# Issuing GpSimd's row transfers without waits on TensorE's steps and without waits for landings

## The chip, the cores and the metric

The kernel runs on one core of a Trainium2 chip. Its time is the device time of one execution, in microseconds (us). Three runs of the kernel before gave 802.45, 809.31 and 810.42 us; their median, 809.31 us, is the time before.

## What is computed

The input x holds 16 sequences of 256 rows with 128 features. Four stages follow one another, each added to x and each fed with a layer norm of x:

```
x = x + attn_a(layernorm(x))      # one head of width 128: softmax(q k^T / sqrt(128)) v, then w_o
x = x + ffn(layernorm(x))         # mixture of experts, layer 0
x = x + attn_b(layernorm(x))      # 16 heads of width 8, causal, with biases
x = x + ffn(layernorm(x))         # mixture of experts, layer 1

# ffn, over N = 4096 rows, E = 8 experts, capacity = 1280 rows an expert
logits = x @ router_w;  gates = softmax(logits)
first and second choice of each row; its place in an expert is a running count over the rows
expert_in = the rows of each expert;  h = silu(expert_in @ w1 + b1);  expert_out = h @ w2 + b2
out = gated sum of a row's two expert rows + 0.1 * (silu(x @ sw1 + sb1) @ sw2 + sb2)
```

## The kernel before

Each engine has a program of its own, written out by hand. The engines meet at semaphores, and each engine works through its list in order, so that a wait holds up all that stands behind it on the same engine.

**The rows.** The 4096 rows are 32 tiles of 128 (`NT`). A pair is two sequences, so four tiles, and there are eight pairs (`PAIRS`). Routing is done pair by pair: VectorE takes the statistics of the second norm (`stats2_end`, L1464), GpSimd makes the inverse deviation (`rstd2_of`, L561 and L563), VectorE writes the normed rows to `xr` (`norm_r`, L1476), TensorE transposes them (`r_transpose`, L808) and makes the logits (L815), VectorE finds both choices (`lead`, `second`), TensorE counts (`counts`, L826 to L836), and VectorE writes the slot numbers (`placed`, L1543 to L1555).

**The row transfers.** `dispatch(l, k)` is GpSimd's indirect DMA (L580): it sends one tile of 128 rows to the slots in `x_slots`, in DRAM, that `slot_u` names. Each pair has eight (four tiles, two choices), so each layer has 64, numbered k from 0 to 63. At every eighth it waits for `placed` of that pair. At the fifth of each eight it waits until the first-choice rows of the pair before have landed.

**Attention A.** TensorE, ScalarE and VectorE go through rounds, a pair in each (`attn_a_pair`). In round i the rows of pair i-2 get their places. GpSimd's list for the rounds 2 to 7 is in `attn_a`: seven transfers a round (four in round 2), each behind a wait for a step of TensorE in that round (`probs_tr` L788, `gv_done` L771, `y_done` L798), and then `rstd2_of(i + 1)`, whose result the next steps of VectorE need. This leaves 25 of the 64 transfers for the time after the attention.

**The layer of experts.** `moe` has items of 256 rows. The first ten in layer 0 and nine in layer 1 (`FRONT`) are pieces of the shared part, which take nothing from `x_slots`. Behind them come 40 chunks of the experts. SyncE's `chunk_loads` waits for all 64 transfers to land, and only then loads the first five chunks into `xg` (L370). TensorE transposes a chunk (`x_tr`, L889), VectorE splits it into a high and a low part (`x_split`, L1662 and L1664), and TensorE multiplies (`first_mm` L918, `second_mm` L939).

**Waits for landings.** `landed(l, k)` holds GpSimd until transfer k is in DRAM. `bursts(l, first, upto, size)` puts one behind every `size` transfers: in layer 0 from transfer 39 to 47 in fours, that is behind 42 and behind 46. In layer 1, where GpSimd is busy with the causal masks until transfer 39 and then sends 40 to 63, they stand behind 42 and behind 47 (`landed(1, 6 * 8 - 1)`), and `rstd2_of(2 * PAIRS)`, the norm of the last pair, stands behind 43.

Of the kernel before, what the change touches and what calls it, by code (L numbers as in the profile page):

```python
# [16 lines left out]
SEQS, SEQ, D = 16, 256, 128  # L17
T = SEQS * SEQ
NT = T // P
PAIRS = SEQS // 2  # L20
# [65 lines left out]
def build(nc, x_in, hd_mask, w_q, w_k, w_v, w_o, attn_W, attn_b, out_W, out_b, router_w,  # L86
          w1, b1, w2, b2, sw1, sb1, sw2, sb2, out):
    with ExitStack() as ctx:
# [93 lines left out]
        S = Signals()  # L182
# [121 lines left out]
        slots2 = (S.slots2_even, S.slots2_odd)  # L304
# [160 lines left out]
        def _(pool):  # L465
# [31 lines left out]
            def key_masks():  # L497

                rows = bdk[96:P, 0, 0, 0, 0:P]
                pool.memset(rows.bitcast(F32), -2.0 ** (KEY_EXP + STEP * SPAN)).then_inc(S.key_mask, 1)  # L500

                for m in range(SPAN, 0, -1):
                    pool.wait_ge(S.key_mask, SPAN - m + 1)
                    pool.affine_select(out=rows, in_=rows, compare_op=ALU.is_ge, pattern=[[1, P]], channel_multiplier=-SPAN,
                                       base=4 * SPAN - m, fill=-2.0 ** (KEY_EXP + STEP * (m - 1)) if m > 1 else 0.0).then_inc(S.key_mask, 1)
                pool.wait_ge(S.key_mask, SPAN + 1)
                pool.affine_select(out=rows, in_=rows, compare_op=ALU.is_ge, pattern=[[0, P]], channel_multiplier=1,
                                   base=-4, fill=0.0).then_inc(S.key_mask, 1)
                pool.wait_ge(S.key_mask, SPAN + 2)
                pool.tensor_copy(bdk[96:P, 0, 0, 0, P:SEQ], rows).then_inc(S.key_mask, 1)  # L510
                pool.wait_ge(S.key_mask, SPAN + 3)
                pool.tensor_copy(bdk[96:P, 0, 0, 1:4, :], bdk[96:P, 0, 0, 0:1, :].broadcast_to([32, 3, SEQ])).then_inc(S.key_mask, 1)
                pool.wait_ge(S.key_mask, SPAN + 4)

            def key_ones():

                for j in range(4):
                    pool.affine_select(out=bdk[96:P, 0, 0, j, :], in_=bdk[96:P, 0, 0, j, :], compare_op=ALU.not_equal,
                                       pattern=[[0, SEQ]], channel_multiplier=1, base=-j, fill=1.0).then_inc(S.key_mask, 1)
                    pool.wait_ge(S.key_mask, SPAN + 5 + j)  # L520

            def query_masks():

                rows = qc[96:P, 0, 0, 0:P]
                pool.memset(rows.bitcast(F32), 0.0).then_inc(S.query_mask, 1)
                for l in range(SPAN):
                    pool.wait_ge(S.query_mask, l + 1)
                    pool.affine_select(out=rows, in_=rows, compare_op=ALU.not_equal, pattern=[[1, P]], channel_multiplier=-SPAN,
                                       base=4 * SPAN - l, fill=2.0 ** (QUERY_EXP - STEP * l)).then_inc(S.query_mask, 1)
                pool.wait_ge(S.query_mask, SPAN + 1)  # L530

            def rstd_of(q, n):

                pool.wait_ge(S.ln_mv, n)
                pool.tensor_scalar(ve[:, 4 * q:4 * q + 4], mv[:, 4 * q:4 * q + 4, 1], EPS, 1.0, ALU.add, ALU.mult).then_inc(S.ln_ve, 1)
                pool.wait_ge(S.ln_ve, n)
                pool.tensor_tensor(rstd[:, 4 * q:4 * q + 4], ve[:, 4 * q:4 * q + 4], neg_half[:, :], ALU.pow).then_inc(S.ln_rstd, 1)
# [18 lines left out]
            def rstd2_of(n):  # L556
                pool.wait_ge(S.ln2_mv, n)
                if n > PAIRS + 1:

                    pool.wait_ge(S.xn2_ready, n - 1)  # L560
                pool.tensor_scalar(ve2[:, :], mv2[:, :, 1], EPS, 1.0, ALU.add, ALU.mult).then_inc(S.ln2_ve, 1)  # L561
                pool.wait_ge(S.ln2_ve, n)
                pool.tensor_tensor(rstd2[:, :], ve2[:, :], neg_half[:, :], ALU.pow).then_inc(S.ln2_rstd, 1)  # L563

            def dispatch(l, k):

                q, c, j = k // 8, k % 8 // 4, k % 4
                n, t = PAIRS * l + q, 4 * q + j
                if k % 4 == 0:
                    if c == 0:  # L570
                        pool.wait_ge(S.placed, PLACED * (n + 1))
                    elif n > 0:

                        pool.wait_ge(slots2[(n - 1) % 2], 64 * ((n - 1) // 2 + 1))
                if k == 0:
                    if l == 0:
                        pool.wait_ge(S.slots_zeroed, 16)
                    else:
                        pool.wait_ge(S.xg_tr, NCH)
                pool.indirect_dma_start(x_slots, bass.IndirectOffsetOnAxis(ap=slot_u[:, c, t:t + 1], axis=0),  # L580
                                        xr[:, t, :], None, bounds_check=E * CAP - 1, oob_is_err=False
                                        ).then_inc(S.slots1 if c else slots2[n % 2], 16)

            def landed(l, k):

                q, c, j = k // 8, k % 8 // 4, k % 4
                n = PAIRS * l + q
                if c:
                    pool.wait_ge(S.slots1, 512 * l + 64 * q + 16 * (j + 1))
                else:  # L590
                    pool.wait_ge(slots2[n % 2], 64 * (n // 2) + 16 * (j + 1))

            def bursts(l, first, upto, size):

                for k in range(first, upto):
                    dispatch(l, k)
                    if (k - first) % size == size - 1 and k + 1 < upto:
                        landed(l, k)

            def scatter(l, c):  # L600
                g = NCH * l + c
                pool.wait_ge(S.yo_ready, item_of_chunk(l, c) + 1)
                pool.wait_ge(S.row_set, g + 1)
                if c == 0:
                    if l == 0:

                        pool.wait_ge(S.bdk_zeroed, 16)
                    else:
                        pool.wait_ge(S.y_used, PAIRS)
                for j in range(CH):  # L610
                    pool.indirect_dma_start(y_rows, bass.IndirectOffsetOnAxis(ap=row_cur[:, g % ROWS, j:j + 1], axis=0),  # L611
                                            yo[:, g % RING, j, :], None, bounds_check=2 * T - 1, oob_is_err=False
                                            ).then_inc(sca[g % RING], 16)

            def attn_a():
                rstd_of(0, 1)
                pool.wait_ge(S.const_pool, N_CONST_POOL)
                pool.wait_ge(S.ln_rstd, 1)
                key_masks()
                rstd_of(1, 2)  # L620
                pool.wait_ge(S.ln_rstd, 2)
                key_ones()
                query_masks()
                for q in range(2, 7):
                    rstd_of(q, q + 1)
                rstd2_of(1)
                rstd_of(7, 8)
                rstd2_of(2)
                k = 0

                def row():
                    nonlocal k
                    dispatch(0, k)
                    k += 1


                for i in range(2, PAIRS):
                    n = 2 * i
                    if i > 2:
                        pool.wait_ge(S.probs_tr, n + 1)  # L640
                        row()
                        pool.wait_ge(S.gv_done, min(n + 3, SEQS))
                        row()
                    pool.wait_ge(S.y_done, n + 1)
                    row()
                    pool.wait_ge(S.probs_tr, n + 2)
                    row()
                    pool.wait_ge(S.gv_done, min(n + 4, SEQS))
                    row()
                    pool.wait_ge(S.y_done, n + 2)  # L650
                    row()
                    if i > 2:
                        row()
                    rstd2_of(i + 1)

                bursts(0, k, 6 * 8, 4)
                for k in range(6 * 8, 2 * NT):
                    dispatch(0, k)

            def attn_b_consts():  # L660
                pool.wait_ge(S.wb_in, 16 * WB_LOADS)
# [56 lines left out]
            for i in range(-1, PAIRS):  # L718
                k = attn_b_pair(i)

            rstd2_of(2 * PAIRS - 1)
            causal(PAIRS - 1, 1, GRP - 2)
            causal(PAIRS - 1, 1, GRP - 1)
            bursts(1, k + 1, k + 5, 3)
            rstd2_of(2 * PAIRS)
            for k in range(k + 5, 6 * 8):
                dispatch(1, k)
            landed(1, 6 * 8 - 1)
            for k in range(6 * 8, 2 * NT):
                dispatch(1, k)  # L730
            for c in range(NCH):
                scatter(1, c)
# [1322 lines left out]
```

## Time and profile before

| | |
|---|---|
| median of three runs | 809.31 us (802.45 to 810.42) |
| the profiled execution | 807.04 us, its span 805.3 us |
| TensorE matmuls | 724.6 us busy, 90% of the span, 6280 instructions |
| TensorE weight loads | 658.5 us, 82% |
| VectorE | 498.8 us, 62% |
| ScalarE | 444.4 us, 55% |
| GpSimd | 443.2 us, 55%, 564 instructions |
| row transfers, L580 | 128, 131.1 us, mean 1024 ns; idle before them 53.0 us |
| TensorE's granted clock, mean of the span | 0.964 of full speed |

The span is what the profiler saw from the first to the last instruction; the execution's own time is 1.7 us longer. Attention A fills the first 104 us or so, the experts of layer 0 stand between 104 and 317 us, attention B follows until about 591 us, and the experts of layer 1 run to the end. TensorE is busy for nine tenths of the span, so what matters is where it stands still, and for whom.

### The profile page before, as it was taken

Reading aid. Unit: us, or ns where it says so; the run is one execution under the profiler, and the core shown is the slowest. Engines: PE = TensorE matmul, PEld = TensorE weight load, DVE = VectorE, ACT = ScalarE, POOL = GpSimd, SP = SyncE. Lnnn points to the kernel's source line nnn. Section 1 sums busy time; section 2 is a strip of 40 time slices with the busy share of each in tenths; the row PEclk is TensorE's granted clock in tenths of the full one; section 3 lists DMA queues with packets and bytes.
Section 4 is the critical chain, followed back from the end, with each engine's and each line's share of the span. In section 5 each row is a group of like instructions: output and inputs, shape, how many; then the busy total and the mean of one; then the engine's idle time right before and its main releaser. Section 6 shows DMA issues by size and latency. Waiting matters only on the chain. (4 is left out here: it accounts for less than half of the span.)

```text
span 805.3 us, 18389 instructions
## 1 busy us (share of the span) xinstructions
PE 724.6 (90%) x6280; PEld 658.5 (82%) x6280; DVE 498.8 (62%) x1594; ACT 444.4 (55%) x1135; POOL 443.2 (55%) x564
## 2 busy tenths in 40 slices
PE   5888789699999997799999889999899799999994
PEld 4777689699999997577777677776689699999994
DVE  4877665245444446678888988877665345444437
ACT  2555345244444442587877877877555244444456
POOL 7367766155555562154454776776757155555530
PEclk9999869899999999899999999999989899999999
DMA  7896111233334223434423432333001233333138
GB/s 257 304 294 159 46 40 50 71 103 102 97 96 121 78 77 105 132 97 122 125 87 112 149 120 90 97 116 105 33 29 50 77 94 96 101 109 113 53 101 231
DMA packets 82723, 89.34 MB, mean 111 GB/s; under 512 B 13016, under 2 KB 70970, under 8 KB 82536
## 3 DMA queue, kind: packets, MB, share of 16 engines
q1 hardware_dynamic: 72432, 70.56, 29.8%
q0 software_dynamic: 9216, 17.34, 6.4%
q8 instruction: 51, 0.84, 0.4%
q10 hardware_dynamic: 984, 0.29, 0.2%
q14 instruction: 40, 0.33, 0.1%
HBM read 49.63 MB, written 39.67 MB: 111 GB/s over the span
## 5 line engine op out<-in xcount | busy, mean ns | idle before, releaser
L1277 ACT ACTIVATE hT<-bank,bias_T 128x256 f32<-128x256 f32 x448 | 175.4, 475 | 213.7 <-PE bank L918 213.7
L611 POOL DMA_INDIRECT y_rows<-yo,row_cur x160 | 157.7, 985 | 144.5 <-DVE yo L1787 117.7
L580 POOL DMA_INDIRECT x_slots<-xr,slot_u x128 | 131.1, 1024 | 53.0 <-issue 33.0
L1874 DVE TENSOR_REDUCE negp<-bank 128x2 f32<-128x512 f32 (+1 forms) x192 | 129.5, 685 | 46.2 <-PE bank L984 27.2
L939 PE MATMUL bank<-w_s,hT 128*128 128x128 f32 x1280 | 155.9, 275 | 0.0
L939 PEld LDWEIGHTS bank<-w_s,hT 128*128 128x128 f32 x1280 | 150.0, 192 | 0.0
L918 PE MATMUL bank<-xT_hl,w_hl 128*128 128x256 f32 x960 | 136.2, 292 | 1.1 <-DVE xT_hl L1664 1.1
L681 POOL TENSOR_SCALAR_AFFINE_SELECT pt<-pt 128x512 f32<-128x512 f32 x128 | 85.8, 678 | 92.8 <-ACT pt L1338 92.5
L1338 ACT ACTIVATE pt<-bank 128x512 f32<-128x512 f32 x192 | 107.7, 596 | 42.2 <-PE bank L1005 40.4
L1787 DVE TENSOR_TENSOR yo<-bank,b_b 128x256 f32<-128x256 f32 x80 | 33.9, 424 | 146.5 <-PE bank L939 146.5
L918 PEld LDWEIGHTS bank<-xT_hl,w_hl 128*128 128x128 f32 x960 | 121.5, 193 | 1.9 <-issue 1.9
L939 PE MATMUL bank<-sw_s,hT 128*128 128x128 f32 x512 | 64.1, 279 | 1.6 <-issue 1.4
L1024 PE MATMUL bank<-pt,v_ext 128*32 128x256 f32 (+1 forms) x1024 | 56.5, 339 | 8.2 <-POOL pt L681 8.1
L939 PEld LDWEIGHTS bank<-sw_s,hT 128*128 128x128 f32 x512 | 61.3, 196 | 2.4 <-issue 2.4
L918 PE MATMUL bank<-xT_hl,sw_hl 128*128 128x256 f32 x384 | 56.7, 300 | 2.9 <-issue 2.4
L918 PEld LDWEIGHTS bank<-xT_hl,sw_hl 128*128 128x128 f32 x384 | 51.0, 202 | 3.9 <-issue 3.2
L1024 PEld LDWEIGHTS bank<-pt,v_ext 128*32 128x32 f32 x1024 | 27.2, 111 | 29.9 <-POOL pt L681 11.6
L983 PE MATMUL bank<-bdk,qc 96*128 96x256 f32 x128 | 49.1, 383 | 0.9 <-DVE negp L1874 0.4
L1662 DVE CAST xT_hl<-bank 128x256 fp32r<-128x256 f32 x80 | 33.1, 414 | 17.9 <-PE bank L889 17.9
L979 PE MATMUL bank<-bdk,qc 128*128 128x512 f32 x64 | 31.5, 491 | 12.0 <-DMA qc<-qk_rows 11.8
L889 PE MATMUL bank<-ident,xg 128*128 128x128 f32 x160 | 31.6, 281 | 11.5 <-DMA xg<-x_slots 11.4
L1001 PE MATMUL bank<-qc,bdk 128*128 128x256 f32 x256 | 41.4, 284 | 0.0
(209 smaller groups left out, 1205.5 us busy)
## 6 DMA issues: line engine op xcount, KB each, us to landing
xg<-x_slots SPq DMA_DIRECT2D x80, 136.0 KB, 2.1
w_s<-in_L_ffn_w SPq DMA_DIRECT2D x32, 256.0 KB, 3.1
qk_rows<-qks SPq DMA_DIRECT2D x16, 512.0 KB, 3.7
bdk<-qk_rows SPq DMA_DIRECT2D x192, 32.0 KB
qc<-qk_rows SPq DMA_DIRECT2D x48, 128.0 KB, 2.9
x_slots<-xg SPq DMA_DIRECT2D x1, 5440.0 KB, 21.4
y_rows<-xg SPq DMA_DIRECT2D x1, 4096.0 KB, 15.7
yab<-y_rows SPq DMA_DIRECT2D x16, 256.0 KB, 3.4
```

The costliest lines, as they stand in the source:

```text
L580: pool.indirect_dma_start(x_slots, bass.IndirectOffsetOnAxis(ap=slot_u[:, c, t:t + 1], axis=0), xr[:, t, :], None, bounds_check=E * CAP - ...
L611: pool.indirect_dma_start(y_rows, bass.IndirectOffsetOnAxis(ap=row_cur[:, g % ROWS, j:j + 1], axis=0), yo[:, g % RING, j, :], None, bounds ...
L681: a = pool.affine_select(out=blk, in_=blk, compare_op=ALU.is_ge, fill=0.0, base=0, pattern=[[0, 4], [1, P]], channel_multiplier=-1)
L918: m = pe.matmul(bk[:, (f % 2) * 256:(f % 2) * 256 + 256], wt[:, wp, f * P:(f + 1) * P], xT_hl[:, w % 2, xp, :], start=(p == 0), stop=(p == 2))
L939: m = pe.matmul(yb(w, l)[:, j * P:(j + 1) * P], hT[:, w % 2, f, j * P:(j + 1) * P], wt[:, f, :], start=(f == 0), stop=(f == FT - 1))
L983: pe.matmul(halves[:, :, 0:P], q[0:96], heads[0:96, :, 0:P], start=True, stop=True)
L1001: m = pe.matmul(bk[:, j * SEQ:j * SEQ + SEQ], bdk[:, par, g, 2 * k + j, 0:P], qc[:, par, g, :], start=True, stop=True)
L1024: m = pe.matmul(OB[32 * j:32 * j + 32, c0 + kt * P:c0 + SEQ], v_ext[:, par, kt, 4 * g + j, :], rhs, start=(kt == 0 and g % 2 == 0), stop=( ...
L1277: a = act.activation(hT[:, w % 2, f, :], HB[2 * (w % 2) + f // 2][:, (f % 2) * 256:(f % 2) * 256 + 256], ACT.Silu, bias=bias_T[:, b0 + f:b ...
L1338: act.activation(pt[:, g % 2, k, :], CB[(g + k) % 2][:, :], ACT.Exp).then_inc(S.exp_done, 1)
L1787: dve.tensor_tensor(yo[:, g % RING, :, :], rows, b2_b[:, e:e + 1, :].broadcast_to([P, CH, D]), ALU.add).then_inc(S.yo_ready, 1)
L1874: dve.tensor_reduce(dst, AB[(g + k) % 2][:, :].rearrange("p (j k) -> p j k", j=heads), AX.X, ALU.max, negate=True).then_inc(S.amax_done, 1)
```

## The change

In attention A the seven transfers of a round follow one another, with no wait for TensorE between them; the number of transfers a round, and the place of `rstd2_of` behind them, stay. After the rounds, the remaining 25 transfers of layer 0 go out with no wait for a landing. In layer 1 both waits for landings go, and five transfers in place of four stand ahead of the last `rstd2_of`. The waits inside `dispatch` (for `placed`, and for the first-choice rows of the pair before) stay.

```diff
-            def landed(l, k):
...
-            def bursts(l, first, upto, size):
...
                 for i in range(2, PAIRS):
-                    n = 2 * i
-                    if i > 2:
-                        pool.wait_ge(S.probs_tr, n + 1)
-                        row()
-                        pool.wait_ge(S.gv_done, min(n + 3, SEQS))
-                        row()
-                    pool.wait_ge(S.y_done, n + 1)
-                    row()
-                    pool.wait_ge(S.probs_tr, n + 2)
-                    row()
-                    pool.wait_ge(S.gv_done, min(n + 4, SEQS))
-                    row()
-                    pool.wait_ge(S.y_done, n + 2)
-                    row()
-                    if i > 2:
+                    for _ in range(7 if i > 2 else 4):
                         row()
                     rstd2_of(i + 1)
-
-                bursts(0, k, 6 * 8, 4)
-                for k in range(6 * 8, 2 * NT):
-                    dispatch(0, k)
+                while k < 2 * NT:
+                    row()
...
             rstd2_of(2 * PAIRS - 1)
             causal(PAIRS - 1, 1, GRP - 2)
             causal(PAIRS - 1, 1, GRP - 1)
-            bursts(1, k + 1, k + 5, 3)
+            for k in range(k + 1, k + 6):
+                dispatch(1, k)
             rstd2_of(2 * PAIRS)
-            for k in range(k + 5, 6 * 8):
-                dispatch(1, k)
-            landed(1, 6 * 8 - 1)
-            for k in range(6 * 8, 2 * NT):
+            for k in range(k + 1, 2 * NT):
                 dispatch(1, k)
```

What GpSimd's list is in one round of attention A (round 3, transfers 4 to 10, and the norm behind them) before:

```order
L580 DMA x_slots<-xr,slot_u 10240x136 [waits probs_tr]
L580 DMA x_slots<-xr,slot_u 10240x136 [waits gv_done]
L580 DMA x_slots<-xr,slot_u 10240x136 [waits y_done]
L580 DMA x_slots<-xr,slot_u 10240x136 [waits probs_tr]
L580 DMA x_slots<-xr,slot_u 10240x136 [waits placed,gv_done]
L580 DMA x_slots<-xr,slot_u 10240x136 [waits y_done]
L580 DMA x_slots<-xr,slot_u 10240x136
L561 TENSOR_SCALAR ve<-mv 128x4 [waits ln2_mv]
L563 TENSOR_TENSOR rstd<-ve,neg_half 128x4 [waits ln2_ve]
```

And the same round in the changed kernel:

```order
L580 DMA x_slots<-xr,slot_u 10240x136 x4
L580 DMA x_slots<-xr,slot_u 10240x136 [waits placed]
L580 DMA x_slots<-xr,slot_u 10240x136 x2
L561 TENSOR_SCALAR ve<-mv 128x4 [waits ln2_mv]
L563 TENSOR_TENSOR rstd<-ve,neg_half 128x4 [waits ln2_ve]
```

The same seven transfers stand ahead of the same norm; of their waits only that for the places of the next pair is left.

GpSimd's list at the end of attention B, from transfer 40 of layer 1 (the first row) to transfer 51 (the last), before:

```order
L580 DMA x_slots<-xr,slot_u 10240x136 [waits placed]
L580 DMA x_slots<-xr,slot_u 10240x136 x2
L580 DMA x_slots<-xr,slot_u 10240x136 [waits slots2_odd]
L561 TENSOR_SCALAR ve<-mv 128x4 [waits xn2_ready,ln2_mv]
L563 TENSOR_TENSOR rstd<-ve,neg_half 128x4 [waits ln2_ve]
L580 DMA x_slots<-xr,slot_u 10240x136 [waits slots2_even]
L580 DMA x_slots<-xr,slot_u 10240x136 x3
L580 DMA x_slots<-xr,slot_u 10240x136 [waits placed,slots1]
L580 DMA x_slots<-xr,slot_u 10240x136 x3
```

And in the changed kernel, to transfer 51 as well:

```order
L580 DMA x_slots<-xr,slot_u 10240x136 [waits placed]
L580 DMA x_slots<-xr,slot_u 10240x136 x3
L580 DMA x_slots<-xr,slot_u 10240x136 [waits slots2_even]
L561 TENSOR_SCALAR ve<-mv 128x4 [waits xn2_ready,ln2_mv]
L563 TENSOR_TENSOR rstd<-ve,neg_half 128x4 [waits ln2_ve]
L580 DMA x_slots<-xr,slot_u 10240x136 x3
L580 DMA x_slots<-xr,slot_u 10240x136 [waits placed]
L580 DMA x_slots<-xr,slot_u 10240x136 x3
```

The waits on `slots2_odd` and `slots1`, which are those for the landing of transfers 42 and 47, are gone, and transfer 44 (the one that waits on `slots2_even`) has moved ahead of the norm.

## Rows read from the trace of the kernel before

**Rows 1.** Waits of TensorE over the whole span: total, times, longest in us.

```profile
PE bank L889 <- DMA xg<-x_slots: 11.4, 2, 6.1
```

**Rows 2.** Timeline of GpSimd, one round of attention A: start, duration, work [idle before].

```profile
49.75 0.20 POOL L561 TENSOR_SCALAR ve<-mv 128x4 f32<-128x4 f32 x1 [1.13 <-DVE mv L1464]
...
57.12 0.97 POOL L580 DMA_INDIRECT x_slots<-xr,slot_u  x1 [0.90 <-PE bank L771]
...
60.71 0.20 POOL L561 TENSOR_SCALAR ve<-mv 128x4 f32<-128x4 f32 x1
```

**Rows 3.** Timeline of TensorE: the counts, one set a round of attention A.

```profile
50.06 0.23 PE L826 MATMUL bank<-base_row,ones_bf 128*128 128x128 bf16 x1 [0.68 <-DVE acc L1534]
...
60.81 0.23 PE L826 MATMUL bank<-base_row,ones_bf 128*128 128x128 bf16 x1 [0.69 <-DVE acc L1534]
...
71.78 0.23 PE L826 MATMUL bank<-base_row,ones_bf 128*128 128x128 bf16 x1 [0.69 <-DVE acc L1534]
```

**Rows 4.** Timeline of VectorE at the statistics and norms of attention A.

```profile
49.28 0.38 DVE L1464 BATCH_NORM_AGGREGATE mv<-st 128x2 f32<-128x6 f32 x4
...
60.02 0.38 DVE L1464 BATCH_NORM_AGGREGATE mv<-st 128x2 f32<-128x6 f32 x4
...
62.06 0.35 DVE L1476 TENSOR_SCALAR xr<-x,mv,rstd 128x128 f32<-128x128 f32 x1 [0.46 <-POOL rstd L563]
...
62.85 0.52 DVE L1476 TENSOR_SCALAR xr<-x,mv,rstd 128x128 f32<-128x128 f32 x1
```

**Rows 5.** Timeline of GpSimd after attention A: transfers 42, 43, 47 and 63 of layer 0.

```profile
111.90 0.97 POOL L580 DMA_INDIRECT x_slots<-xr,slot_u  x1 [0.30 <-issue]
115.24 0.97 POOL L580 DMA_INDIRECT x_slots<-xr,slot_u  x1 [2.36 <-DMA x_slots<-xr,slot_u]
...
122.63 0.97 POOL L580 DMA_INDIRECT x_slots<-xr,slot_u  x1 [2.08 <-DMA x_slots<-xr,slot_u]
...
143.34 0.97 POOL L580 DMA_INDIRECT x_slots<-xr,slot_u  x1 [0.30 <-issue]
```

**Rows 6.** Timeline of TensorE at the first chunk of layer 0.

```profile
147.88 1.52 PE L889 MATMUL bank<-ident,xg 128*128 128x128 f32 x4 [6.10 <-DMA xg<-x_slots]
149.81 2.90 PE L918 MATMUL bank<-xT_hl,w_hl 128*128 128x256 f32 x12 [0.41 <-DVE xT_hl L1664]
```

**Rows 7.** Timeline of GpSimd, layer 1: transfer 43, the last norm, transfer 48.

```profile
594.71 0.96 POOL L580 DMA_INDIRECT x_slots<-xr,slot_u  x1 [2.10 <-DMA x_slots<-xr,slot_u]
595.75 0.20 POOL L561 TENSOR_SCALAR ve<-mv 128x4 f32<-128x4 f32 x1
...
604.91 0.96 POOL L580 DMA_INDIRECT x_slots<-xr,slot_u  x1 [2.08 <-DMA x_slots<-xr,slot_u]
```

**Rows 8.** The chain that ended last, layer 1: start, us, what.

```profile
624.65 2.28 DMA x_slots<-xr,slot_u
...
631.00 2.90 PE bank L918 x12
633.90 2.38 PE bank L939 x16
...
636.49 1.44 PE bank L918 x12
637.93 1.79 PE bank L939 x16
```

**Rows 9.** Timeline of VectorE: slot numbers of pair 7 (layer 0) and pair 6 (layer 1).

```profile
121.20 0.15 DVE L1555 TENSOR_TENSOR slot_u<-RR,far 128x4 uint32<-128x4 f32 x1
...
599.96 0.16 DVE L1555 TENSOR_TENSOR slot_u<-RR,far 128x4 uint32<-128x4 f32 x1
```

**Rows 10.** Windows: length, busy of PE, PEld, DVE, ACT, POOL, clock, DMA share, GB/s.

```profile
15.40:17.50 2.10, 0.01 (x1) 0.00 (x0) 2.06 (x13) 1.57 (x6) 1.48 (x6) 1.00 1.01 412
...
94.70:97.00 2.30, 1.79 (x15) 1.50 (x15) 2.06 (x11) 1.02 (x4) 2.07 (x2) 0.72 0.00 0
...
141.80:147.80 6.00, 0.00 (x0) 0.00 (x0) 0.00 (x0) 0.00 (x0) 1.95 (x2) 0.93 0.25 77
```

More of the change, by code:

```diff
@@ L582, in dispatch @@
                                         ).then_inc(S.slots1 if c else slots2[n % 2], 16)
-            def landed(l, k):
[L586 to L591, printed above, removed]
-            def bursts(l, first, upto, size):
[L595 to L598, printed above, removed]
             def scatter(l, c):
```

## The prediction

> **What bounds the kernel now.** I read the waits of TensorE first, since it is busy for 90% of the span. Two of its waits are for the load of a first chunk: 11.4 us in two pieces, 6.1 us in layer 0 and the other 5.3 us in layer 1 [rows 1]. Then the chain that ended last: in layer 1 it goes back from the end of the experts through the load to the landing of the last row transfer, and from there up GpSimd's list of transfers [rows 8]. So GpSimd's last transfer sets when the experts start, and behind the start TensorE runs with no gap until the tail. In layer 0 the same pattern stands in the timelines: transfer 63 is issued at 143.34 us, and TensorE starts the first chunk at 147.88 us after 6.10 us of standing still [rows 5, 6]. Last I looked at whether GpSimd also holds up the rounds of attention A, where its norm stands behind seven transfers.
>
> **Waits on TensorE's steps.** One of them costs: the fifth transfer of a round stands 0.90 us, where the usual gap is 0.30 us, so 0.60 us a round [rows 2, 5]. That is GpSimd's time, and it counts only if the norm behind the transfers is late. It is, a little: VectorE's statistics end at 60.02 + 0.38 = 60.40 us, and GpSimd starts the norm at 60.71 us, while in the round before, where GpSimd was waiting, it started 0.09 us after them (49.28 + 0.38 against 49.75) [rows 2, 4]. So it is 0.31 - 0.09 = 0.22 us late, and VectorE waits 0.46 us for it [rows 4]. TensorE's rounds show the same number: 60.81 - 50.06 = 10.75 us with a norm in time, 71.78 - 60.81 = 10.97 us with a late one [rows 3]. Without the 0.60 us GpSimd is ready at about 60.11 us, before the statistics, and the round is VectorE's and TensorE's again at 10.75 us. Three rounds have a late norm (starts at 60.71, 71.68 and 82.64 us); the last two rounds are paced by other work. Sum: 3 x 0.22 = 0.7 us. Bounds: 0 if the rounds find another pace at 10.97 us, 1.4 us if the 0.46 us of VectorE's wait went in all three. What is late next is the statistics.
>
> **Waits for landings, layer 0.** Transfer 43 stands 2.36 us and transfer 47 2.08 us [rows 5]. With the usual 0.30 us in their place, 2.06 + 1.78 = 3.84 us go. Nothing takes their place: the only wait left in this stretch that could come last is that of transfer 56 for the slots of pair 7, which are written at 121.20 us [rows 9], and transfer 56 goes out seven transfers ahead of 63, so at about 134 us before and 130 us after. The shared pieces of TensorE end at 147.88 - 6.10 = 141.78 us, and shift with attention A by the same 0.7 us as GpSimd does. So the standing still falls from 6.10 to 2.26 us, all 3.84 us are gained, and 2.26 us of cover are not there to be used up: had the saving been over 6.1 us, the rest would have been lost.
>
> **Waits for landings, layer 1.** Transfer 43 stands 2.10 us and transfer 48 2.08 us [rows 7]: 1.80 + 1.78 = 3.58 us. The transfer that is moved ahead of the last norm costs 1.27 us there (0.97 + 0.30), against the 1.80 us that are gone ahead of it, so the norm starts some 0.5 us earlier, and no later, than at 595.75 us. Transfer 48 would go out at about 601.3 us; the slots that it waits for are written at 599.96 us [rows 9], so this wait does not come up. TensorE's standing still falls from 5.3 to 1.7 us. The row transfers of both layers sum to 7.4 us.
>
> **The clock after the standing still.** In layer 0 the granted clock was at 1.00, and fell to 0.50 (1.2 GHz) near the end of the 6 us without a matmul (mean 0.93 over 141.8 to 147.8 us) [rows 10]. The first chunk then ran slowly: in layer 1 its two products took 2.90 and 2.38 us on the chain, the next chunk's 1.44 and 1.79 us, so 1.46 + 0.59 = 2.05 us more [rows 8]; layer 0 shows the same 2.90 us [rows 6]. If the clock stays at 2.4 GHz through 2.3 and 1.7 us, that comes back, about 1.9 us a layer (2.05, less since layer 0's second product overlaps a little more). At 15.4 us TensorE stood still for 2.10 us, and the clock was 1.00 throughout [rows 10]. Against it: in attention A it fell to a mean of 0.72 at 94.7 to 97.0 us, in a slack stretch [rows 10]; and here the transposes of the first chunk and VectorE's split follow the gap, in which TensorE does little for 1.93 us (147.88 to 149.81) [rows 6]. So the bounds are 0 and 4.1 us. I take both, 3.8 us, as the likeliest single case, being nearest to the row with the same length of gap.
>
> **The sum.** 0.7 + 3.84 + 3.58 + 3.8 = 11.9 us. The profiled execution took 807.04 us (span 805.3), which gives 795.1 us. The median of the runs lies 2.3 us higher, which gives 797.4 us by the same sum; I forecast 796. From the fastest run, 802.45, it would be 790.5.
>
> **A page against the trace.** A transfer starts behind each norm of GpSimd's, while VectorE norms the rows, and it shows: the third TENSOR_SCALAR took 0.52 us in place of 0.35 [rows 4]. The Trainium skill (SBUF — State Buffer, section "SBUF: two separate sides") says that GpSimd and VectorE's instructions in a two-port mode take a shared pair of ports as an exclusive lock, so that the loser stands until the other has ended. By that rule an instruction that meets a transfer would stand up to 0.97 us, and the sum would turn into the loss worked out under the third rival; by the row it stands 0.2 us, and the sum stays.
>
> **Rival 1: the clock falls all the same.** In both layers: 0.7 + 3.84 + 3.58 = 8.1 us, 799 us from the profiled execution and 801 from the median. In one layer: 10 us, 797 to 799. For it speak the slack stretch in attention A and the split behind the gap; against it the gap at 15.4 us.
>
> **Rival 2: the landing grows with the row.** If transfers sent back to back wait for one another in the DMA queue, the last lands no earlier and only attention A's 0.7 us is left: 806 to 808.5 us. For it: transfer 42 took 115.24 - 111.90 = 3.3 us until GpSimd went on [rows 5]. Against it: transfer 63 of layer 1, after fifteen others without such a wait, landed in 2.28 us [rows 8], so no queue had built up. The same time comes if the freed waits turn up again inside GpSimd's issue.
>
> **Rival 3: slower, because VectorE meets the transfers.** The waits keep the middle transfers of a round behind steps of TensorE, while VectorE works on PSUM; without them they may fall on its norms. A round has eight TENSOR_SCALAR of this kind, four for each norm. If each stood for half a transfer, 0.49 us, a round would be 3.9 us longer, five rounds 19.5 us, and the time would be 807 - 11.9 + 19.5 = 815 us. It turns the sign from 11.9 / 5 = 2.4 us a round, 0.3 us for each of the eight. The row of 0.52 us shows 0.17 us in one of four [rows 4], and GpSimd is sending for nine of eleven microseconds already, so there is little room for more meetings.
>
> **The chances.** Both clocks stay: 0.38. One falls: 0.27. Both fall: 0.15. Rival 2: 0.13. Rival 3: 0.07. The range takes in both ends of the clock's case from the fastest run to the median, 790 to 801, and a part of what lies between rival 1 and rival 2: 789.5 to 804. A measurement of this kernel can tell about 1%, 8 us, from no change. The first two cases are faster by more than that (0.65), a third of rival 1's double case too (0.05); the rest of it, rival 2 and a little of rival 3 are within 1% (0.25); slower by over 1% is 0.05.
>
> **What the changed profile would show.** Right: no transfer of layer 0 or 1 that waits on DMA by more than 0.3 us; GpSimd's waits on TensorE gone, and its norm waiting some 0.4 us for the statistics; TensorE's counts 10.75 us apart in four rounds; TensorE's waits for the chunk load at about 2.3 and 1.7 us; the first `first_mm` of the experts near 1.7 us where the clock stayed up. Wrong: gaps of 5 to 6 us ahead of the first chunk with an earlier last transfer (rival 2); transfers of more than 1.3 us or TENSOR_SCALAR of more than 0.6 us in many rounds, with rounds over 11 us (rival 3); a clock of 0.50 behind gaps of 2 us (rival 1). The prediction would also be wrong if the clock in attention A, which before shows a mean of 0.72 at 94.7 to 97.0 us [rows 10], falls at another place: more may hang on that than on the 0.7 us that the change brings there.

## The result and the profile after

| | |
|---|---|
| before, beside it on the same chip | 809.26 us, median of six (802.45 to 810.42) |
| changed | 796.36 us, median of six (795.37 to 800.91) |
| ratio | 0.986, 95% interval 0.983 to 0.989: 9.1 to 14.1 us faster; the medians are 12.9 us apart |
| profiled execution of the changed kernel | 800.91 us, span 799.2 us, the slowest of its six |

The forecast was 796.0 us with a range of 789.5 to 804. Since the profiled execution is the slowest of its six, its rows show less of the gain than the median. I read it in the order of the prediction: the waits of TensorE, attention A, the two ends of the row transfers, the clock.

Waits of TensorE over the whole span: total, times, longest in us. This answers to [rows 1], where the same wait was 11.4 us.

```profile
PE bank L854 <- DMA xg<-x_slots: 5.7, 2, 2.9
```

It has halved, and the chain that ended last still goes through it in layer 1. In the list of the costliest groups GpSimd's transfers are as long as before, and only the idle time ahead of them has shrunk, from 53.0 to 40.0 us; nearly all that is left is the usual gap between two of them (122 gaps, 34.3 us in all):

```profile
L580 POOL DMA_INDIRECT x_slots<-xr,slot_u x128 | 131.3, 1026 | 40.0 <-issue 34.3
```

Attention A, first GpSimd's timeline (start, duration, work, idle before), a round's last transfer and the norm behind it, as in [rows 2]:

```profile
61.09 0.97 POOL L580 DMA_INDIRECT x_slots<-xr,slot_u  x1 [0.30 <-issue]
62.51 0.20 POOL L561 TENSOR_SCALAR ve<-mv 128x4 f32<-128x4 f32 x1 [0.45 <-DVE mv L1429]
```

GpSimd now stands 0.45 us and waits for VectorE's statistics, where the norm was late before. TensorE's counts, as in [rows 3]:

```profile
52.08 0.23 PE L791 MATMUL bank<-base_row,ones_bf 128*128 128x128 bf16 x1 [0.69 <-DVE acc L1499]
...
62.83 0.23 PE L791 MATMUL bank<-base_row,ones_bf 128*128 128x128 bf16 x1 [0.69 <-DVE acc L1499]
...
73.58 0.23 PE L791 MATMUL bank<-base_row,ones_bf 128*128 128x128 bf16 x1 [0.70 <-DVE acc L1499]
```

They are 10.75 us apart, and so is the next. VectorE's norms, as in [rows 4], and behind them the transfer that GpSimd sends at that time:

```profile
63.87 0.35 DVE L1441 TENSOR_SCALAR xr<-x,mv,rstd 128x128 f32<-128x128 f32 x1 [0.24 <-POOL rstd L563]
...
64.65 0.52 DVE L1441 TENSOR_SCALAR xr<-x,mv,rstd 128x128 f32<-128x128 f32 x1
...
64.03 1.12 POOL L580 DMA_INDIRECT x_slots<-xr,slot_u  x1 [0.20 <-issue]
```

The wait for the norm fell from 0.46 to 0.24 us. Three of the four start inside the transfer's 1.12 us, at 64.32, 64.65 and 64.98 us: as before one of them took 0.52 us, the other two 0.34 us each.

GpSimd after attention A: the last norm of the stage, and transfer 63, as in [rows 5]. The first line is the same norm before:

```profile
106.22 0.20 POOL L561 TENSOR_SCALAR ve<-mv 128x4 f32<-128x4 f32 x1
...
107.63 0.20 POOL L561 TENSOR_SCALAR ve<-mv 128x4 f32<-128x4 f32 x1 [1.37 <-DVE mv L1429]
...
140.81 1.01 POOL L580 DMA_INDIRECT x_slots<-xr,slot_u  x1 [0.30 <-issue]
```

From the norm to transfer 63 it is 33.18 us; before, it was 143.34 - 106.22 = 37.12 us. No transfer between them waits for a landing. TensorE at the first chunk of layer 0, as in [rows 6]:

```profile
145.90 0.96 PE L854 MATMUL bank<-ident,xg 128*128 128x128 f32 x4 [2.77 <-DMA xg<-x_slots]
147.59 2.23 PE L883 MATMUL bank<-xT_hl,w_hl 128*128 128x256 f32 x12 [0.72 <-DVE xT_hl L1629]
...
152.45 0.38 PE L854 MATMUL bank<-ident,xg 128*128 128x128 f32 x2
```

Layer 1, GpSimd, as in [rows 7]: transfer 40 before, and then, of the changed kernel, transfer 40, the last norm, and two of the transfers that took longer than 0.97 us; transfer 63 starts at 617.53 us:

```profile
588.85 1.07 POOL L580 DMA_INDIRECT x_slots<-xr,slot_u  x1 [3.33 <-DVE slot_u L1555]
...
584.79 1.07 POOL L580 DMA_INDIRECT x_slots<-xr,slot_u  x1 [2.19 <-DVE slot_u L1520]
...
591.18 0.20 POOL L561 TENSOR_SCALAR ve<-mv 128x4 f32<-128x4 f32 x1
...
598.58 1.12 POOL L580 DMA_INDIRECT x_slots<-xr,slot_u  x1 [0.30 <-issue]
...
613.21 1.46 POOL L580 DMA_INDIRECT x_slots<-xr,slot_u  x1 [0.31 <-issue]
```

From 40 to 63 it is 32.74 us; before, it was 624.65 - 588.85 = 35.80 us. The chain that ended last (start, us, what), as in [rows 8]:

```profile
617.53 2.29 DMA x_slots<-xr,slot_u
...
619.83 2.19 DMA xg<-x_slots
...
623.76 2.90 PE bank L883 x12
```

and TensorE's own timeline there:

```profile
622.07 1.08 PE L854 MATMUL bank<-ident,xg 128*128 128x128 f32 x4 [2.88 <-DMA xg<-x_slots]
...
626.45 3.49 PE L904 MATMUL bank<-sw_s,hT 128*128 128x128 f32 x16
629.78 0.38 PE L854 MATMUL bank<-ident,xg 128*128 128x128 f32 x2
```

The landing takes 2.29 us as before (2.28), so in layer 1 nothing had queued up behind transfers sent back to back. The first chunk ran slowly in both layers. Windows of layer 0 and layer 1 (length, busy of PE, PEld, DVE, ACT, POOL, clock, DMA share, GB/s), as in [rows 10]:

```profile
143.50:147.00 3.50, 0.88 (x4) 0.41 (x4) 0.52 (x2) 0.00 (x0) 0.00 (x0) 1.00 0.58 166
147.00:150.00 3.00, 2.41 (x14) 2.44 (x15) 1.56 (x6) 0.15 (x1) 0.00 (x0) 0.73 0.38 108
622.00:624.00 2.00, 1.20 (x5) 0.68 (x6) 1.31 (x5) 0.00 (x0) 0.00 (x0) 0.71 0.66 202
624.00:627.00 3.00, 3.00 (x15) 3.00 (x16) 1.49 (x5) 0.31 (x1) 0.00 (x0) 0.50 0.30 73
```

In layer 0 the clock was at 1.00 until the first chunk's transposes had passed and fell within the next 3 us; in layer 1 it was at 0.50 (1.2 GHz) through the first product and the start of the second.

This execution by itself: from the first of TensorE's counts to the end of the span it took 799.2 - 41.38 = 757.8 us, before 805.3 - 39.36 = 765.9 us. That is 8.1 us less, the number of rival 1, and the clock fell in both layers, as in rival 1. But the pieces of the 8.1 us are not the terms of the forecast: 4.0 us go up to the first chunk of layer 0, 2.1 us from there to transfer 40 of layer 1, 2.9 us from that transfer to the first chunk of layer 1, and 0.9 us are lost behind it. The 2.1 us lie in the experts of layer 0 and in attention B, which the change doesn't touch. The nine traces of undisturbed sessions without a filling scatter from 434.9 to 442.4 us in that stretch, and their first count stands anywhere from 38.7 to 42.6 us; here it is 2.0 us later than before. So a single execution can't tell a term of 1 or 2 us by its total.

### The profile page after: what moved, and what is told of

The parts are those of the page before. It is cut to its first block and busy times, and to the rows that moved or that the text cites. A ratio compares the mean times of both kernels' runs of the same rounds, so it can differ in the third digit from the quotient of the medians.

```text
span 799.2 us, 18381 instructions
## 1 busy us (share of the span) xinstructions
PE 724.4 (91%) x6280; PEld 658.6 (82%) x6280; DVE 498.8 (62%) x1594; ACT 444.3 (56%) x1135; POOL 443.4 (55%) x564
## 5 line engine op out<-in xcount | busy, mean ns | idle before, releaser
L580 POOL DMA_INDIRECT x_slots<-xr,slot_u x128 | 131.3, 1026 | 40.0 <-issue 34.3
L1627 DVE CAST xT_hl<-bank 128x256 fp32r<-128x256 f32 x80 | 33.1, 414 | 11.6 <-PE bank L854 11.6
L948 PEld LDWEIGHTS bank<-bdk,qc 96*128 96x128 f32 x128 | 26.0, 203 | 17.3 <-issue 9.0
```

Of the source, the lines that this page charges most:

```text
L948: pe.matmul(halves[:, :, 0:P], q[0:96], heads[0:96, :, 0:P], start=True, stop=True)
```

## The experiments

Kernels that share a chip and a session share the runs of the kernel before. Their medians: first session 807.47 us (31 runs), second 827.88 (11), third 806.88 (11), fourth 806.55 (17).

### Each part alone

`e1_attn_a`: only the waits on TensorE's steps in attention A go.

```diff
-                    n = 2 * i
-                    if i > 2:
-                        pool.wait_ge(S.probs_tr, n + 1)
-                        row()
...
-                    pool.wait_ge(S.y_done, n + 2)
-                    row()
-                    if i > 2:
+                    for _ in range(7 if i > 2 else 4):
                         row()
```

> The kernel before with only attention A's waits on TensorE's steps removed. My theory (the parts add up): three rounds 0.22 us shorter, 0.7 us in all, which a measurement cannot tell from no change (ratio 0.999); in the profile GpSimd's norm waits some 0.4 us for the statistics, TensorE's counts stand 10.75 us apart in four rounds, and the standing still before the first chunk of layer 0 stays at 6.1 us. Rival (VectorE meets the transfers): rounds over 11 us, 1 us or more slower. Rival (these waits carried the gain): 4 us or more faster, with the standing still of layer 0 well under 6 us.

Measured: 807.66 us, ratio 1.000 (0.997 to 1.003). The same kernel on another chip in the fourth session:

> Attention A's part alone once more, for a chip where the kernel before takes some 828 us. Theory of the unbroken row (there, transfers that follow one another with nothing between them stall the other engines' issue after some five, and the waits on TensorE's steps keep the row broken): rounds 3 to 6 take 13 to 16 us in place of 11 to 12, some 15 us slower than before, ratio 1.015 to 1.02. Rival (on that chip the rows behind the attention do it): within 3 us of before, counts 11 to 12 us apart. On a chip where the kernel before takes 807 us: 1.000 again.

Measured: 808.57 us, ratio 0.999 (0.996 to 1.002). The traces have counts 10.75 us apart, so the mechanism is there, but its price is under what 24 runs can tell from nothing. The standing still ahead of the first chunk of layer 0, expected to stay at 6.1 us, was 7.51 us in the first and 6.12 us in the second.

`e2_land0`: only the waits for landings in layer 0 go.

```diff
-                bursts(0, k, 6 * 8, 4)
-                for k in range(6 * 8, 2 * NT):
-                    dispatch(0, k)
+                while k < 2 * NT:
+                    row()
```

> The kernel before with only the waits for landings of layer 0 removed. My theory: the standing still before the first chunk of layer 0 falls from 6.1 to 2.3 us, 3.8 us faster, and up to 5.7 where the clock stays up behind it (ratio 0.993 to 0.995); the last transfer lands 2.3 us after its issue. Rival (the landing grows with the row): nothing gained, the last transfer lands later after its issue.

Measured: 800.27 us, ratio 0.992 (0.989 to 0.995). The execution in the profile was the fastest of the twelve (795.54 us). TensorE at the first chunk of layer 0:

```profile
142.59 0.79 PE L888 MATMUL bank<-ident,xg 128*128 128x128 f32 x4 [2.38 <-DMA xg<-x_slots]
144.28 1.67 PE L917 MATMUL bank<-xT_hl,w_hl 128*128 128x256 f32 x12 [0.90 <-DVE xT_hl L1663]
...
147.58 0.38 PE L888 MATMUL bank<-ident,xg 128*128 128x128 f32 x2
```

Here the standing still is 2.38 us and the clock stayed: 1.67 us where before had 2.90. In layer 1 of the same execution, where the waits were kept, it is 5.33 us, and the product took 2.90 us:

```profile
617.72 1.12 PE L888 MATMUL bank<-ident,xg 128*128 128x128 f32 x4 [5.33 <-DMA xg<-x_slots]
619.65 2.90 PE L917 MATMUL bank<-xT_hl,w_hl 128*128 128x256 f32 x12 [0.82 <-DVE xT_hl L1663]
```

`e3_land1`: only the edit of layer 1, the last two pieces of the diff.

```diff
-            bursts(1, k + 1, k + 5, 3)
-            rstd2_of(2 * PAIRS)
-            for k in range(k + 5, 6 * 8):
+            for k in range(k + 1, k + 6):
                 dispatch(1, k)
-            landed(1, 6 * 8 - 1)
-            for k in range(6 * 8, 2 * NT):
+            rstd2_of(2 * PAIRS)
+            for k in range(k + 1, 2 * NT):
                 dispatch(1, k)
```

> The kernel before with only layer 1's part: its waits for landings removed, five transfers ahead of the last norm. My theory: the standing still of layer 1 falls from 5.3 to 1.7 us or, as in the changed kernel's profile, 2.9 us less what VectorE and TensorE give back; 3.6 us faster, up to 5.6 where the clock stays up (ratio 0.993 to 0.996). Rival (the moved transfer and the freed waits turn up in a wait for slot numbers): 1.8 us or less.

Measured: 801.19 us, ratio 0.992 (0.989 to 0.996). Its layer 1:

```profile
624.93 0.99 PE L887 MATMUL bank<-ident,xg 128*128 128x128 f32 x4 [1.48 <-DMA xg<-x_slots]
626.62 1.67 PE L916 MATMUL bank<-xT_hl,w_hl 128*128 128x256 f32 x12 [0.69 <-DVE xT_hl L1662]
```

`e10_landings_only`: both of these edits, attention A as before.

> The waits for landings of both layers removed, attention A's kept. On a chip where the kernel before takes some 828 us: rounds of attention A as before; by the theory of the unbroken row the pauses behind the attention begin earlier, and what the waits give is taken back there, within 4 us of before (0.995 to 1.005); if only attention A's part is harmful there, 7 us or more faster (0.990 or less). On a chip where the kernel before takes 807 us: 7.4 us and some clock, ratio 0.984 to 0.990.

Measured: 798.63 us, ratio 0.989 (0.984 to 0.994). The product of the three parts' ratios is 1.000 x 0.992 x 0.992 = 0.984, that of the whole 0.986, this one 0.989: they agree within their intervals, so the times show no more than a sum of the parts, and no share of attention A's. Its profile has both outcomes of the clock in one execution, layer 0 first:

```profile
145.28 0.99 PE L886 MATMUL bank<-ident,xg 128*128 128x128 f32 x4 [2.30 <-DMA xg<-x_slots]
146.97 1.67 PE L915 MATMUL bank<-xT_hl,w_hl 128*128 128x256 f32 x12 [0.70 <-DVE xT_hl L1661]
...
620.75 0.90 PE L886 MATMUL bank<-ident,xg 128*128 128x128 f32 x4 [2.79 <-DMA xg<-x_slots]
622.43 2.61 PE L915 MATMUL bank<-xT_hl,w_hl 128*128 128x256 f32 x12 [0.78 <-DVE xT_hl L1661]
...
627.27 0.38 PE L886 MATMUL bank<-ident,xg 128*128 128x128 f32 x2
```

### More of the suspected wait

`e6_more_landings`: the kernel before, with four waits for landings in place of two in layer 0.

```diff
-                bursts(0, k, 6 * 8, 4)
+                bursts(0, k, 6 * 8, 2)
```

> The kernel before with waits for landings behind every second transfer of layer 0's nine in place of every fourth: four waits in place of two. My theory (GpSimd's list is the chain, a wait costs 1.9 us): the standing still of layer 0 grows from 6.1 to 9.9 us, 3.8 us slower (ratio 1.005). Rival (a wait costs only where the queue is full, or is hidden): under 1 us.

Measured: 811.54 us, ratio 1.006 (1.003 to 1.008), so 4.4 us (2.0 to 6.8). In its trace GpSimd stands 2.09, 2.24, 2.09 and 2.08 us at the four waits, and TensorE 8.98 us ahead of the first chunk, against 6.10 [rows 6] and the 9.9 expected. Two more waits cost 4.4 us, near the 3.8 us that the forecast gives to two fewer, with the clock low behind the gap in both kernels (first product 2.90 us); this is the cleanest support for the main step.

### The changed kernel again, and the second session

`e0_after_again`: the changed kernel as it is.

> The changed kernel once more, beside the next kernels on one chip: ratio to the kernel before of 0.983 to 0.989 as in its own runs.

Measured: 840.85 us (832.86 to 846.87) against 827.88 (822.07 to 831.04) of the kernel before, ratio 1.014 (1.009 to 1.019). In the second session both kernels were slower than in any other, and the changed one was the slower of the two. One round of attention A, GpSimd:

```profile
71.46 0.97 POOL L580 DMA_INDIRECT x_slots<-xr,slot_u  x1 [0.30 <-issue]
77.90 0.20 POOL L561 TENSOR_SCALAR ve<-mv 128x4 f32<-128x4 f32 x1 [5.46 <-DVE mv L1429]
```

The transfers are as fast as ever, but the norm waits 5.46 us for the statistics; the counts stand at 50.10, 63.61, 79.04, 95.10 and 110.51 us, rounds of 13.5 to 16.1 us where the usual one has 10.75. The waits of TensorE, and below them its timeline in the pieces of the shared part:

```profile
PE bank L904 <- issue: 11.0, 14, 2.8
PE bank L883 <- issue: 10.0, 10, 1.9
```

```profile
136.34 0.55 PE L883 MATMUL bank<-xT_hl,sw_hl 128*128 128x256 f32 x3 [1.03 <-issue]
...
143.46 1.09 PE L904 MATMUL bank<-sw_s,hT 128*128 128x128 f32 x3 [1.03 <-issue]
```

TensorE runs a few matmuls and stands still for about a microsecond, over and over, and no engine or DMA that it waits for is shown ("issue"). In the usual profile the same two groups stand for 3.3 and 1.3 us in the whole span.

The wait for the first chunk does not occur in this execution, in neither layer. In layer 0 TensorE ends the shared pieces so late that it goes on to the chunk at 177.34 us without standing still, 17.0 us after transfer 63 (160.37 us); in the usual profiles the load is there 4.5 to 5.1 us after that transfer's start. What the earlier last transfer could give was not to be had here. The three other profiles of the session show no such wait either; the kernel before was not profiled in it.

`e7_rows_ahead` (changed kernel, 5, 7, 7, 7, 8, 8 transfers in the rounds in place of 4 and five times 7):

```diff
-                    for _ in range(7 if i > 2 else 4):
+                    for _ in range((5, 7, 7, 7, 8, 8)[i - 2]):
```

> The changed kernel with more transfers in the rounds of attention A: 5, 7, 7, 7, 8, 8 in place of 4, 7, 7, 7, 7, 7, so that 22 and not 25 are left behind it; GpSimd stood 1.9 us in round 2 and 1.4 us in round 7 waiting for the statistics. My theory (GpSimd's last transfer sets the start of the experts until the 2.8 us of standing still are used up): the standing still of layer 0 goes, 2.8 us less, and 1.6 us more from the clock; ratio to before 0.980 to 0.983. Rival (a transfer in a round delays the norm, and the rounds grow by 1 us each): no gain over the changed kernel or slower, with TensorE's counts more than 12 us apart in the last rounds.

Measured in the second session: 834.15 us, ratio 1.003 (0.998 to 1.009): in the disturbed session not told from the kernel before, and by the two ratios 1% better than the changed kernel (1.003 against 1.014).

`e4_after_fill` (changed kernel) and `e5_before_fill` (kernel before, with 44 in place of 16) keep TensorE multiplying the identity, into a bank that nobody reads, while it would stand still:

```diff
                     if c == -1:
+                        pe.wait_ge(S.yo_ready, ITEMS * l + 3)
+                        keep_busy(16)
                         x_tr(l, 0)
```

> The changed kernel with 16 matmuls of the identity on TensorE ahead of the first chunk's transposes in both layers (their result is written over), which fill most of the 2.8 us in which it stands still. Theory of the clock (what the change gained beyond the 8.1 us of waits is the clock that stays up in some executions; where it falls it costs 1.6 to 3 us a layer): the clock stays at 1.00 at both places, the first chunk's products take about 1.7 and 2.0 us, and the time is 1 to 4 us under the changed kernel's, near its fastest runs (795 us), with a narrower spread. Rival (the extra gain came from elsewhere): the same as the changed kernel within 0.5 us, though the clock stays up.

> The kernel before with 44 such matmuls at the same two places, filling most of the 6.1 and 5.3 us. Theory of the clock: 2 us less in each layer, some 4 us faster than the kernel before (ratio 0.995), at an unchanged standing time for the load. Rival (the clock's fall costs nothing, since the first chunk is bound by something else): no change.

Measured in the second session: 846.12 us, ratio 1.023 (1.019 to 1.027), and 851.66 us, ratio 1.030 (1.027 to 1.034). Neither tells of the clock here: in the second session there was no gap to fill, so that the filling came on top (3.6 us a layer in the one, 9.8 us in the other). But `e5_before_fill` has the waits of the kernel before, and its trace was taken beside that of the changed kernel: its counts go from 42.58 to 111.06 us in six rounds, 68.5 us, where those of `e0_after_again` go from 39.39 to 122.59 us, 83.2 us. The other two kernels without the waits of attention A agree with the latter: 82.5 us in `e4_after_fill`, 81.5 us in `e7_rows_ahead`. Yet TensorE pauses in `e5_before_fill` too. In layer 0 nearly all of it stands between 135 and 150 us, in the last transfers, which go out unbroken in both kernels; over the span its two groups of products stand for 26.9 us in 22 pauses, more than the 21.0 us of the changed kernel:

```profile
147.27 1.48 PE L939 MATMUL bank<-sw_s,hT 128*128 128x128 f32 x5 [3.25 <-issue]
```

### The same two in an undisturbed session

`e7b_rows_ahead`:

> The kernel with 5, 7, 7, 7, 8, 8 transfers in the rounds of attention A once more, hoping for a chip where the kernel before takes 807 us as in the first runs. My theory there: ratio to before 0.980 to 0.983, the standing still of layer 0 gone, TensorE's counts 10.75 us apart. If the chip is one where the kernel before takes some 828 us: near 1.003 again, with pauses of TensorE put down to issue.

Measured: 792.38 us (788.78 to 797.1) against 806.88, ratio 0.981 (0.977 to 0.984), the lowest ratio of all. Its interval just touches that of the changed kernel (0.983 to 0.989). Transfer 63 goes out at 138.16 us, and in layer 0 the wait for the chunk is all but gone:

```profile
143.78 0.44 PE L854 MATMUL bank<-ident,xg 128*128 128x128 f32 x2 [0.52 <-DMA xg<-x_slots]
144.50 1.67 PE L883 MATMUL bank<-xT_hl,w_hl 128*128 128x256 f32 x12 [0.29 <-DVE xT_hl L1629]
...
147.80 0.38 PE L854 MATMUL bank<-ident,xg 128*128 128x128 f32 x2
```

GpSimd's norm still waits 0.64, 0.46, 0.45, 0.45 and 0.15 us for the statistics in the rounds 2 to 6 and no longer in round 7: the rounds had room for just these three transfers.

`e4b_after_fill`:

> The changed kernel with 16 filling matmuls ahead of the first chunk in each layer once more. Theory of the clock, on a chip where the kernel before takes 807 us: the clock stays at 1.00 behind the gap in both layers, 1 to 4 us less than the changed kernel, ratio to before 0.981 to 0.986. Rival: 0.986 with the clock up, since the extra gain came from elsewhere.

Measured: 799.13 us, ratio 0.987 (0.984 to 0.991), where 0.981 to 0.986 was expected.

```profile
143.16 3.74 PE L704 MATMUL bank<-ident 128*128 128x128 f32 x32
146.73 0.60 PE L854 MATMUL bank<-ident,xg 128*128 128x128 f32 x4
148.36 1.66 PE L883 MATMUL bank<-xT_hl,w_hl 128*128 128x256 f32 x12 [1.03 <-DVE xT_hl L1631]
```

The clock stayed at 1.00 in both layers (1.66 us for the first product, in layer 1 too), so in this execution filling the gap was enough to keep it. The time did not fall below that of the changed kernel: the filling lasts 3.6 us to the first transpose, longer than the gap. The first chunk starts 146.73 - 139.37 = 7.4 us after the last transfer's start, against 145.90 - 140.81 = 5.1 us in the changed kernel; in layer 1 it is 5.1 against 4.5 us. Not all of the 2.3 us in layer 0 is the filling's doing: SyncE issued the load 4.28 us after the start of transfer 63, against 2.92 us in the changed kernel. The 0.6 to 2.3 us lost in a layer are of the size of what the clock gives back there (2.0 us, worked out below), and the runs, 794.0 to 801.5 us, scatter no less than those of the changed kernel.

## Why the prediction was right

**Waits for landings, layer 0.** Forecast 3.84 us, measured 37.12 - 33.18 = 3.94 us on GpSimd. By itself the part brings 6.5 us of time (ratio 0.992; 4.3 to 8.6), the wait and the clock together; the forecast for both was 5.7 us. The gap left was 2.77 us in the profiled execution, forecast 2.26; 2.30 and 2.38 us in two others. The 0.5 us lies behind transfer 63: from its start to the first transpose it is 145.90 - 140.81 = 5.09 us, before 147.88 - 143.34 = 4.54 us. SyncE issued the load 2.92 us after the transfer's start, before 2.41 us, and from the issue to the first transpose it is 2.2 and 2.1 us. Why the issue came later is open; in three other traces with the same transfers sent back to back (`e2_land0`, `e10_landings_only`, `e7b_rows_ahead`) it came after 2.40 to 2.46 us, so the missing waits alone don't explain it.

**Waits for landings, layer 1.** Forecast 3.58 us, measured 3.06: the waits are gone, but more transfers than before took 1.12 or 1.46 us in place of 0.97, as rows above show, and gave 0.5 us back. TensorE's pieces ended 0.5 us earlier too, counted from transfer 40, so the gap left was 2.88 us and not 1.7. With the same list it was 2.79 us in `e10_landings_only`, and 1.48 and 1.52 us in `e3_land1` and `e7b_rows_ahead`, where transfers 40 to 63 took 32.0 and 31.9 us. The part alone brings 0.992 (3.1 to 9.3 us); forecast 5.5.

**Attention A.** Forecast 0.7 us. The traces show the step: a norm that waits 0.45 us, counts at 10.75 us, 78.56 us from the first to the last count against 79.21. The time doesn't show it; two runs of the part alone gave 1.000 and 0.999.

**The clock.** The size of this term was right, and it went into the sum in full without being certain. I set 1.9 us a layer as if a gap of about 2 us kept the clock. The profiles, by the gap ahead of the first chunk: with 0.52, 1.48, 1.52, 2.30 and 2.38 us the first product took 1.67 us (clock at 2.4 GHz), with 2.77 us 2.23, with 2.79 us 2.61, and with 2.88 us 2.90; from 5.3 to 9.0 us it took 2.90 each time that it wasn't cut up in the record. What a kept clock gives back stands between the first chunk's transposes and those of the next chunk. Before:

```profile
154.88 0.38 PE L889 MATMUL bank<-ident,xg 128*128 128x128 f32 x2
...
629.06 1.23 PE L889 MATMUL bank<-ident,xg 128*128 128x128 f32 x4 [5.30 <-DMA xg<-x_slots]
...
636.11 0.38 PE L889 MATMUL bank<-ident,xg 128*128 128x128 f32 x2
```

So before it was 154.88 - 147.88 = 7.00 us in layer 0 and 7.05 us in layer 1. Where the clock stayed it is 147.58 - 142.59 = 4.99 us (`e2_land0`): 2.0 us a layer, the 1.9 forecast. Behind the three gaps of 2.77 to 2.88 us it is 6.55, 6.52 and 7.71 us, so the changed kernel's profiled execution won 0.4 us in layer 0, lost 0.7 us in layer 1 and got nothing of the term in all. All three gaps of that length were followed by a fall, so it isn't shown that the changed kernel ever kept the clock; its gap in layer 1 did vary by more than a microsecond in kernels with the same list there.

**The number.** The median gained 12.9 us, or 11.6 by the ratio, and the sum was 11.9. That the two are so near is in part luck. By the forecast's account the five runs that weren't profiled kept the clock in one layer or both, and no trace shows that. What is on record of them is the mean granted clock: 0.979, 0.976, 0.974 and 0.972 in the four fastest (795.4 to 797.1 us), 0.970 and 0.969 in the two slowest (799.3 and 800.9 us). It fits, but the mean doesn't say where the clock fell, and the kernel before scatters more widely (802.7 to 813.6 us in the first session), with gaps of a length behind which the clock fell in every trace. Of the 4.5 us between the profiled run and the median, 2.0 us may be the late first count.

**The rivals.** Rival 1 is what the profiled execution did with the clock; the median lies nearly 5 us below the 801 us that rival 1 gives for it, and no trace shows what the clock did in the other runs. Rival 2 is out: transfers sent back to back land in 2.29 us in layer 1, and the gaps ahead of the first chunks shrank. Rival 3 is out where nothing else disturbed the chip: VectorE's norm took 0.52 us as before and the rounds 10.75 us. The Trainium skill (SBUF — State Buffer, "SBUF: two separate sides") has one of GpSimd and a VectorE instruction in a two-port mode stand for the other's whole instruction. No run shows in which mode these norms ran; what the rows show is that three of them started inside a transfer of 1.12 us and took 0.34, 0.52 and 0.34 us, so VectorE does not stand for a whole transfer. In one session the changed kernel did come out slower, by 1.4%, but not by that mechanism: the norms' TENSOR_SCALAR has a median of 341 ns there, against 344 ns in the usual profile; TensorE's issue paused.

**What stays open.** What disturbed the second session. Its chip had the same number as that of the third, in which before took 806.88 us, so it is not fixed to that number. I can say what the traces show: pauses of TensorE with no releaser, in stretches where transfers go out unbroken, and rounds over 2 us longer (81.5 to 83.2 against 68.5 us over six) in the three kernels that had lost the waits. That the removed waits had shielded attention A in such a condition fits all four traces, but the kernels differ in more than that, and the part alone was not measured in that condition: `e1b_attn_a` was meant for it and came in an undisturbed session.

## What to carry to other kernels

When one engine's list ends in the instruction that starts the next stage, a wait in that list costs about its full length, even if the stage's own engine is busy for 90% of the span; look for the gap at the stage's start and follow it back. Where there is no such gap, as in the second session, an earlier last instruction brings nothing. Moving such work into rounds that have slack (three transfers more, until the norm was just in time) gave the lowest ratio, 0.981 of before against 0.986. The clock adds about 2 us for each gap at TensorE that becomes short enough: here it stayed behind all five gaps of 2.4 us and less and fell behind the three of 2.77 to 2.88 us, so a forecast that lands near these lengths should carry the term as a chance and not as a sum. And measure on more than one occasion, since a change that packs transfers closer was 1.4% faster in one session and 1.4% slower in another.

## What the runs showed of the hardware that I had not expected

- A condition of a whole session, in which this kernel took 828 us in place of 807, with GpSimd's transfers at their usual 0.97 us, while in the changed kernel TensorE's issue paused 24 times for 21.0 us in two groups that otherwise show 4.6 us. The granted clock's mean was 0.94 to 0.96 in the changed kernel's runs there, against 0.97 to 0.98 in its first ones.
- With the clock at 1.00 through the gap it can still fall just after it, within the first product: a stretch of 3.5 us at 1.00, then 0.73 over the next three.
- An indirect transfer of 128 rows on GpSimd takes 0.97 us, but now and then 1.12 or 1.46; in layer 1 this cost the changed kernel 2.0 us in 24 transfers, 0.5 us more than before.
